# Attention with part of its exponentials on VectorE: a polynomial shared with GpSimd, and 30 key tiles instead of 27

## The chip, the cores and the metric

The kernel runs on one core of a Trainium2 chip. A core has TensorE (PE, with its weight loads as PEld), ScalarE (ACT), VectorE (DVE), GpSimd (POOL) and SyncE (SP, which issues DMAs). The metric is the device time of one execution in microseconds (us), given as the median of the runs.

## The reference

A cross-attention of 1024 queries over 6404 keys, 16 heads of 8 channels, and then a small mixture of experts. What matters here, cut down:

```
q = (layernorm(x) @ Wq + bq)          # 1024 x 128, 16 heads of 8
k, v = ctx @ Wk + bk, ctx @ Wv + bv   # 6404 x 128
attn = softmax(clip(q @ k.T * 8**-0.5, -1e4, 1e4))
x = x + (attn @ v) @ Wo + bo
x = x + a * (gelu(ln(x) @ W1m + b1m) @ W2m + b2m) + (1 - a) * experts(ln(x))
```

The work is in exp over 16 x 1024 x 6404 scores.

## The kernel before

The context is transposed and projected first, until about 53 us. Then comes the attention loop. It has eight passes; a pass is one group of four heads and one half of the queries (512 columns). The keys form 50 full tiles of 128 and a tail of 4. A (pass, key tile) is a step of four chunks, one for each head, of 128 keys by 512 queries. Three chunks make a tile of the loop: TensorE computes their scores into one of two PSUM tensors `ps` (L1058, the four heads in four row groups of the array), ScalarE takes exp of all 1536 columns in one instruction (L514), and TensorE adds the values of the steps that are complete (L1122, the four heads beside each other) into the pass's bank `po`. So in three of four tiles there is a values step and in one there is none. Two tiles of scores are in flight.

Some steps go to VectorE instead, by a list written out in the code, `D_PLAN`: pass, key tile, the four tiles of the loop at which TensorE makes the score of one head (a "spare score", in the `po` bank that the running pass doesn't use), the order of the heads, and the tile at which the values are added. VectorE makes exp by range reduction and a polynomial of degree five in three factors. For each spare score there is `u` (L764, adds a magic number and so rounds) and `f` (L767, the remainder), 512 columns each, after which the bank is free (`spare_taken`). Two scores make a pair of 1024 columns, on which `pair_until` runs six stages: 1 `e`, the shift of u into an exponent (L783); 2 `q1` = (f + A1) f (L792, and once for each key tile `vd`, L790); 3 `q2` = (f + A2) f (L794); 4 `p1` = (q1 + B1) e (L797); 5 `p2` = (q2 + B2) p1 (L800); 6 the last, (f - R0) p2 (L803), which signals `d_ready`. The stages of a pair are laid between u and f of the next pair's scores (`split_exponent`). TensorE must not make a spare score before VectorE has taken the one before it (`spare_job`, wait on `spare_taken`), and as its queue is in order, score tiles and values wait behind that.

At the end of a pass VectorE copies the sums out (`take_sums`, L746), TensorE transposes them into the spare bank (L1080, a "token job" in the same list of spare jobs), and VectorE divides (`normalise`, L738 and L739). Before, the pair begun is carried to stage 6 ahead of that. After pass 6 the first half of the queries is finished during pass 7: projection, layer norm, first main layer (`first_half_main`).

GpSimd has nothing to do in the loop but the power that gives the layer norm's rstd of the first half (L471). In the tail TensorE and VectorE hand each other the second half: transposes (L1151), normalise (L739), transposes (L1014), projection (L1021), residual and statistics, rstd by GpSimd, xn (L583), transposes (L1028), first layers (L1197), and `second_layer(0, 0)`, the second main layer of the first half, after the projection and ahead of L1028 (L1224, L1216).

The loop stands in an If on a range flag; its Else is a general path that these inputs don't take.

## Time and profile before

| | us |
|---|---|
| median of 3 runs | 810.94 |
| lowest, highest | 809.8, 810.98 |
| profiled execution | 812.0 |
| its span, first to last instruction | 810.3 |
| mean granted TensorE clock | 0.985 |

| engine | busy us | share of the span |
|---|---|---|
| TensorE matmuls | 732.8 | 90% |
| ScalarE | 726.7 | 90% |
| VectorE | 551.3 | 68% |
| GpSimd | 20.7 | 3% |

Busy time is not time on the path. A matmul's end is modelled and matmuls overlap, so TensorE's share says little; what tells is who waits for whom, and how long the engine that is waited for leaves no gap.

### The profile page before, as it was taken

What the parts mean: (1) busy time and instruction counts of PE and PEld (TensorE: products, weight loads), DVE (VectorE), ACT (ScalarE), POOL (GpSimd) and SP (SyncE); (2) the same over time, 40 slices, a digit from 0 to 9 for tenths busy, and PEclk for the clock granted to TensorE, in tenths of its full rate; (3) what the DMA queues carried; (4) which work ended last, traced back from release to release, by engine and by line L of the source; (5) the groups of instructions that cost most, each with busy time, mean ns of one, the idle gap of its engine ahead of it and who ended that gap; (6) DMA issues with size and microseconds to landing.
All of it is one profiled execution on the core that took longest, in us unless ns stands there. A gap on an engine that the chain in (4) does not pass through costs nothing.

```text
span 810.3 us, 13099 instructions
## 1 busy us (share of the span) xinstructions
PE 732.8 (90%) x5386; PEld 217.2 (27%) x5386; DVE 551.3 (68%) x760; ACT 726.7 (90%) x587; POOL 20.7 (3%) x36
## 2 busy tenths in 40 slices
PE   5988899999998998999989999899899999998798
PEld 3642222222222222222212222222222222222457
DVE  5634499798877988699759977898769884100220
ACT  3769999999999998999979999999899998999451
POOL 8000000000000000000000000000000000000000
PEclk9989999999999999999999999999999999999999
DMA  5259110011110000111100000111100000000010
GB/s 186 104 151 291 57 42 1 26 42 33 34 34 1 1 2 10 40 33 34 50 1 1 2 1 18 49 33 33 34 1 2 1 1 1 1 1 1 4 53 27
DMA packets 15325, 29.05 MB, mean 36 GB/s; under 512 B 2439, under 2 KB 5885, under 8 KB 15261
## 3 DMA queue, kind: packets, MB, share of 16 engines
q1 hardware_dynamic: 13562, 26.86, 10.8%
q8 instruction: 45, 0.74, 0.4%
q10 hardware_dynamic: 1218, 0.64, 0.3%
q0 software_dynamic: 480, 0.66, 0.3%
q14 instruction: 20, 0.16, 0.1%
HBM read 20.02 MB, written 8.13 MB: 35 GB/s over the span
## 4 chain that ended last, share of the span: by engine, by line
PE 47%; ACT 21%; issue 18%; DVE 8%; DMA 4%; SPq 1%; POOLq 0%; POOL 0%; DVEq 0%; ACTq 0%
PE po L1122 25%; ACT region_ctxT L514 20%; PE ps L1058 13%; DMA k_dram<-kparts 3%; PE ps L1197 2%; PE po L1216 1%; PE ps L950 1%; DVE dres L800 1%; DVE dres L797 1%; PE po L961 1%; DMA region_ctx<-in_ctx 1%; PE ps L938 1%; DVE dres L803 1%; DVE xn L583 1%; DVE dres L792 1%
## 5 line engine op out<-in xcount | busy, mean ns | idle before, releaser
L514 ACT ACTIVATE region_ctxT<-ps 128x1536 f32<-128x1536 f32 x500 | 680.0, 1531 | 21.2 <-PE ps L1058 21.0
L1122 PE MATMUL po<-region_ctxT,v 128*9 128x512 f32 x2984 | 393.6, 600 | 0.9 <-ACT region_ctxT L514 0.5
L1058 PE MATMUL ps<-qst,region_k 32*128 32x512 f32 x1492 | 252.9, 496 | 45.7 <-ACT region_ctxT L514 45.1
L1058 PEld LDWEIGHTS ps<-qst,region_k 32*128 32x128 f32 x1492 | 96.8, 182 | 420.4 <-ACT region_ctxT L514 398.9
L764 DVE TENSOR_SCALAR region_kT<-po 128x512 f32<-128x512 f32 x108 | 74.2, 687 | 92.2 <-PE po L1058 92.0
L767 DVE SCALAR_TENSOR_TENSOR region_kT<-region_kT,po 128x512 f32<-128x512 f32 x108 | 73.6, 681 | 0.7
L1122 PEld LDWEIGHTS po<-region_ctxT,v 128*9 128x9 f32 x2984 | 44.4, 88 | 94.2 <-issue 90.8
L803 DVE SCALAR_TENSOR_TENSOR dres<-region_kT,dres 128x1024 f32<-128x1024 f32 x54 | 66.2, 1225 | 1.8
L800 DVE SCALAR_TENSOR_TENSOR dres<-region_kT,dres 128x1024 f32<-128x1024 f32 x54 | 65.9, 1220 | 0.5
L792 DVE SCALAR_TENSOR_TENSOR dres<-region_kT 128x1024 f32<-128x1024 f32 x54 | 65.8, 1218 | 0.0
L794 DVE SCALAR_TENSOR_TENSOR region_kT<-region_kT 128x1024 f32<-128x1024 f32 x54 | 65.8, 1218 | 0.0
L797 DVE SCALAR_TENSOR_TENSOR dres<-dres,region_kT 128x1024 f32<-128x1024 f32 x54 | 65.7, 1216 | 0.0
L1058 PE MATMUL po<-qst,region_k 32*128 32x512 f32 x108 | 53.5, 495 | 3.9 <-DVE xn L739 3.0
L783 DVE TENSOR_SCALAR region_kT<-region_kT 128x1024 uint32<-128x1024 uint32 x54 | 36.9, 683 | 0.0
L746 DVE COPY region_kT<-po 128x512 f32<-128x512 f32 x8 | 5.5, 684 | 39.8 <-PE po L1108 39.8
L1122 PE MATMUL po<-dres,vd 128*9 128x512 f32 x216 | 28.6, 601 | 2.5 <-DVE dres L803 2.5
L1058 PEld LDWEIGHTS po<-qst,region_k 32*128 32x128 f32 x108 | 19.6, 181 | 5.8 <-DVE xn L739 3.4
L471 POOL TENSOR_TENSOR rstd<-rstd,powers 128x4 f32<-128x4 f32 x2 | 2.1, 1027 | 743.7 <-DVE rstd L578 743.7
L938 PE MATMUL ps<-ident,region_ctx 128*96 128x128 f32 x50 | 9.7, 332 | 7.3 <-DMA region_ctx<-in_ctx 7.3
L701 DVE TENSOR_SCALAR region_ctx<-po,b1T 128x512 f32<-128x512 f32 x4 | 3.0, 751 | 19.2 <-PE po L1037 19.2
L358 ACT ACTIVATE region_ctxT<-ps 96x512 f32<-96x512 f32 (+1 forms) x13 | 7.4, 572 | 9.4 <-PE ps L938 9.4
L624 DVE CAST kparts<-region_kT 128x640 fp32r<-128x640 f32 (+1 forms) x10 | 4.9, 493 | 15.4 <-DMA k_dram<-kparts 14.3
(191 smaller groups left out, 304.8 us busy)
## 6 DMA issues: line engine op xcount, KB each, us to landing
region_k<-k_dram SPq DMA_DIRECT2D x40, 320.0 KB, 3.3
k_dram<-kparts SPq DMA_DIRECT2D x18, 320.0 KB, 4.2
qst<-q_dram SPq DMA_DIRECT2D x16, 128.0 KB
region_ctx<-in_ctx SPq DMA_DIRECT2D x2, 624.0 KB, 9.3
q_dram<-region_k SPq DMA_DIRECT2D x2, 512.0 KB, 2.7
k_dram<-kparts SPq DMA_DIRECT2D x2, 322.0 KB, 5.3
region_ctx<-in_ctx SPq DMA_DIRECT2D x1, 576.0 KB, 7.4
xres<-in_x SPq DMA_DIRECT2D x1, 512.0 KB, 4.4
```

The source lines that it names most:

```text
L514: act.activation(probs[:, t % NPR, :], ps[t % NSB][:, :], ACT.Exp, scale=ESCALE).then_inc(exp_ready, 1)
L764: d_count(("u", c), v.tensor_scalar(du[:, i % 2, part], src, MAGIC, None, ALU.add))
L767: v.scalar_tensor_tensor(df[:, i % 2, part], du[:, i % 2, part], MAGIC, src, ALU.subtract, ALU.subtract).then_inc(spare_taken, 1)
L783: d_count(("e", i), v.tensor_scalar(u.bitcast(U32), u.bitcast(U32), 23, None, ALU.logical_shift_left))
L792: d_count(("q1", i), v.scalar_tensor_tensor(res, f, A1, f, ALU.add, ALU.mult))
L794: d_count(("q2", i), v.scalar_tensor_tensor(q, f, A2, f, ALU.add, ALU.mult))
L797: d_count(("p1", i), v.scalar_tensor_tensor(res, res, B1, u, ALU.add, ALU.mult))
L800: d_count(("p2", i), v.scalar_tensor_tensor(res, q, B2, res, ALU.add, ALU.mult))
L803: v.scalar_tensor_tensor(res, f, R0, res, ALU.subtract, ALU.mult).then_inc(d_ready, 1)
L938: last = tr(dst[:, at:at + P], ctx_sb[:, t, :], ident[:, :])
L1058: return mm(dst, kst[r, kt * P:(kt + 1) * P], qst[r, g, queries], start=True, stop=True)
L1122: last = mm(dst[QUAD * j:QUAD * j + V9, :], w, src, start=first, stop=last_one, skip_group_check=True)
```

## The change

Three things in the loop and one in the tail.

- The plan has 30 key tiles on VectorE instead of 27, in passes 0 to 7: 1, 4, 5, 4, 5, 4, 5, 2. The loop has 496 tiles instead of 500. The first spare score is at tile 29 instead of 21; often three tiles lie between two spare scores; two key tiles are in pass 7, the last with scores at tiles 466 to 477 and values at 485. Of the 59 distances between the first scores of one pair and the next, 34 are 6 tiles and six are 5.
- GpSimd makes q1 in two instructions on 1024 columns, `res = f + A1` and `res = res * f`, when both f of a pair are there (`first_factor`, semaphore `factor_ready`). VectorE's p1 waits for it. The power of L471 is placed between the factors.
- Ahead of a token job's normalising, the pair begun is carried on by at most `BETWEEN` = 2 stages and goes on afterwards. `D_GAP`, by which a pair was finished at once where the next score was over 6 tiles away, is gone; only the last pair is finished at once.
- In the tail the second main layer of the first half is cut into its four row tiles (`second_main`): one after the transposes L1151, one after L1014, two after the projection; then ten matmuls of 128 x 128 whose result isn't used (`IDLE`), ahead of the transposes L1028.

```diff
--- before.py
+++ after.py
@@ -60,8 +60,10 @@
 MIX_BANK = 5
 NORM_GAP = 2
 EPI_GAPS = [2, 2, 6, 2, 2, 2, 2]
-D_GAP = 6
+BETWEEN = 2
 OUT_TILES = [(0, QT // 2), (QT // 2, 3 * QT // 4), (3 * QT // 4, QT)]
+
+IDLE = 10
 ALPHA_COL = C + (E + 1) * CB
 assert FULL % NSEG == 0
 
@@ -82,33 +84,36 @@
 
 
 D_PLAN = [
-    (0, 44, (21, 23, 28, 30), (0, 2, 1, 3), 44),
-    (0, 49, (34, 37, 40, 43), (3, 0, 1, 2), 56),
-    (1, 49, (47, 50, 53, 60), (2, 3, 0, 1), 71),
-    (1, 48, (63, 70, 72, 77), (1, 2, 0, 3), 91),
...
-    (6, 47, (405, 408, 411, 418), (2, 3, 0, 1), 430),
-    (7, 49, (420, 425, 427, 433), (3, 2, 0, 1), 449),
+    (0, 49, (29, 31, 34, 36), (0, 2, 3, 1), 48),
+    (1, 49, (39, 42, 45, 52), (2, 3, 0, 1), 71),
+    (1, 48, (55, 58, 61, 64), (2, 3, 0, 1), 79),
+    (1, 47, (70, 72, 75, 81), (2, 0, 1, 3), 91),
+    (1, 46, (84, 87, 90, 93), (0, 1, 2, 3), 107),
+    (2, 14, (96, 99, 102, 105), (0, 1, 2, 3), 134),
...
+    (6, 47, (406, 410, 413, 416), (1, 0, 2, 3), 426),
+    (7, 49, (419, 422, 425, 428), (0, 1, 2, 3), 473),
+    (7, 48, (466, 468, 471, 477), (0, 2, 3, 1), 485),
 ]
 DKT = [[kt for p, kt, *_ in D_PLAN if p == q] for q in range(NP)]
 STEPS = [(p, kt) for p in range(NP) for kt in range(FULL + 1) if kt not in DKT[p]]
@@ -151,8 +156,8 @@
 
 
 def tile_of_segment(p, s):
-    return max(c for c, (n, _) in enumerate(CHUNKS)
-               if STEPS[n][0] == p and (STEPS[n][1] < FULL and STEPS[n][1] // SEG_T == s)) // CPT
+    return max((c for c, (n, _) in enumerate(CHUNKS)
+                if STEPS[n][0] == p and (STEPS[n][1] < FULL and STEPS[n][1] // SEG_T == s)), default=0) // CPT
 
 
 def spare_of_segment(g, s):
@@ -301,6 +306,7 @@
         kst_in = [sem(f"kst_in{s}") for s in range(NSEG)]
         bqs_ready, vtail_ready, powers_ready = sem("bqs_ready"), sem("vtail_ready"), sem("powers_ready")
         spare_psum, spare_taken, d_step, d_ready = sem("spare_psum"), sem("spare_taken"), sem("d_step"), sem("d_ready")
+        factor_ready = sem("factor_ready")
         pre_psum, pre_taken, main0_ready = sem("pre_psum"), sem("pre_taken"), sem("main0_ready")
         bsumb_psum, bsumb_taken = sem("bsumb_psum"), sem("bsumb_taken")
         scores_ready, exp_ready, pv_done, o_taken = sem("scores_ready"), sem("exp_ready"), sem("pv_done"), sem("o_taken")
@@ -465,10 +471,38 @@
             pool.wait_ge(powers_ready, 1)
             pool.memset(euler[:, :], math.e).then_inc(powers_ready, 1)
             pool.wait_ge(powers_ready, 2)
-            for n in range(NHALF):
+
+            first_power = [True]
+
+            def power(n):
                 pool.wait_ge(var_ready, 2 + n)
                 r = slice(n * QT // 2, (n + 1) * QT // 2)
                 pool.tensor_tensor(rstd[:, 3, r], rstd[:, 0, r], powers[:, 0:QT // 2], ALU.pow).then_inc(std_ready, 1)
+
+            def first_factor(i):
+
+                d, half = divmod(i, 2)
+                res = dres[:, d % 2, half * 2 * BANK:(half + 1) * 2 * BANK]
+                pool.wait_ge(spare_taken, SPARE_OF["score", 2 * i + 1] + 1)
+                if d >= 2:
+                    pool.wait_ge(pv_done, VALUES_OF_D[d - 2] + 1)
+                pool.tensor_scalar(res, df[:, i % 2, :], A1, None, ALU.add).then_inc(factor_ready, 1)
+                pool.wait_ge(factor_ready, 2 * i + 1)
+                pool.tensor_tensor(res, res, df[:, i % 2, :], ALU.mult).then_inc(factor_ready, 1)
+
+            pool.wait_ge(flag_ready, 1)
+            safe = pool.value_load(flag[0:1, 0:1], min_val=0, max_val=1)
+            with pool.If(safe != 0):
+                for i in range(len(D_PLAN) * GH // 2):
+                    if SPARE_OF["score", 2 * i + 1] > SPARE_OF["tokens", LAST_OF_HALF[0]] and first_power[0]:
+                        power(0)
+                        first_power[0] = False
+                    first_factor(i)
+                if first_power[0]:
+                    power(0)
+            with pool.Else():
+                power(0)
+            power(1)
             pool.wait_ge(msum_ready, 2)
             pool.tensor_tensor(gate[0:1, 2, :], euler[:, :], gate[0:1, 1, :], ALU.pow).then_inc(exp_gate, 1)
 
@@ -789,11 +823,11 @@
                                 heads = slice(GH * PASSES[p][0], GH * (PASSES[p][0] + 1))
                                 v.tensor_scalar(vd[:, d % 2, :].rearrange("p (h m) -> p h m", m=V9), v9[:, kt, heads, :],
                                                 C5, None, ALU.mult)
-                            d_count(("q1", i), v.scalar_tensor_tensor(res, f, A1, f, ALU.add, ALU.mult))
                         elif d_stage[i] == 3:
                             d_count(("q2", i), v.scalar_tensor_tensor(q, f, A2, f, ALU.add, ALU.mult))
                         elif d_stage[i] == 4:
-                            dve.wait_ge(d_step, max(d_mark["q1", i], d_mark["e", i]))
+                            dve.wait_ge(factor_ready, 2 * (i + 1))
+                            dve.wait_ge(d_step, d_mark["e", i])
                             d_count(("p1", i), v.scalar_tensor_tensor(res, res, B1, u, ALU.add, ALU.mult))
                         elif d_stage[i] == 5:
                             dve.wait_ge(d_step, max(d_mark["p1", i], d_mark["q2", i]))
@@ -807,11 +841,12 @@
                     if kind == "score":
                         split_exponent(i, n)
                         pairs = (i + 1) // 2
-                        if n + 1 == len(SPARE) or SPARE[n + 1][1] == "score" and SPARE[n + 1][0] > SPARE[n][0] + D_GAP:
+                        if pairs == len(d_stage):
                             pair_until(pairs - 1, 6)
                     else:
                         take_sums(i)
-                        pair_until(pairs - 1, 6)
+                        if pairs:
+                            pair_until(pairs - 1, min(6, d_stage[pairs - 1] + BETWEEN))
                         dve.wait_ge(spare_psum, n + 1)
                         ins = normalise(i, po[1 - pv_bank(i + 1)][:, :])
                         ins.then_inc(spare_taken, 1)
@@ -1021,6 +1056,22 @@
                     last = mm(dst[:, i * P:(i + 1) * P], attT[:, t * P:(t + 1) * P], wo_sb[:, :], start=True, stop=True)
                 last.then_inc(y_psum, 1)
 
+            def ffn_sum(t):
+
+                n = max(n for n, (t0, _) in enumerate(OUT_TILES) if t0 <= t)
+                a = t - OUT_TILES[n][0]
+                return [po[0], po[1], bank(4)][n][:, a * P:(a + 1) * P], a == 0
+
+            def second_main(t):
+
+                if t == 0:
+                    pe.wait_ge(main0_ready, 1)
+                    pe.wait_ge(w2_scaled, 1)
+                dst, first = ffn_sum(t)
+                for cb in range(CB):
+                    mm(dst, hid[0][:, cb, t * P:(t + 1) * P], w2m_sb[:, cb, :],
+                       start=(cb == 0 and first), stop=False, skip_group_check=True)
+
             def xn_transpose(n, dst):
 
                 pe.wait_ge(xn_ready, QT + (n + 1) * QT // 2)
@@ -1150,9 +1201,13 @@
                 for a in range(QT // 2):
                     last = tr(bank(0)[:, a * P:(a + 1) * P], oraw[:, (NP - 1) % 2, a * P:(a + 1) * P], ident[:, :])
                 last.then_inc(tok_psum, 1)
+                second_main(0)
                 pe.wait_ge(attention_done, NHALF)
                 att_transpose(1, bank(4))
+                second_main(1)
                 project_out(1, bank(5))
+                for t in range(2, QT // 2):
+                    second_main(t)
             with pe.Else():
                 with pe.Fori(0, H) as h:
                     with pe.Fori(0, QT) as t:
@@ -1186,6 +1241,8 @@
                     first_main(cb)
                 att_transpose(1, bank(4))
                 project_out(1, bank(5))
+                for t in range(QT // 2):
+                    second_main(t)
 
             def first_layer(e, steps):
                 for r in steps:
@@ -1197,17 +1254,8 @@
                     mm(bank(n % 4), w,
                        xnT[:, half * BANK:(half + 1) * BANK], start=True, stop=True).then_inc(hid_psum, 1)
 
-            def ffn_sum(t):
-
-                n = max(n for n, (t0, _) in enumerate(OUT_TILES) if t0 <= t)
-                a = t - OUT_TILES[n][0]
-                return [po[0], po[1], bank(4)][n][:, a * P:(a + 1) * P], a == 0
-
             def second_layer(e, half):
-                if e == 0 and half == 0:
-                    pe.wait_ge(main0_ready, 1)
-                else:
-                    pe.wait_ge(hid_ready, e * CB * NHALF + CB * half)
+                pe.wait_ge(hid_ready, e * CB * NHALF + CB * half)
                 pe.wait_ge(w2_scaled, e + 1)
                 w2 = w2m_sb if e == 0 else w2s[:, e - 1, :, :]
                 for t in range(half * QT // 2, (half + 1) * QT // 2):
@@ -1221,7 +1269,8 @@
                     last.then_inc(ffn2_done, 1)
 
 
-            second_layer(0, 0)
+            for _ in range(IDLE):
+                mm(bank(3, P, P), ident[:, :], ones[:, :], start=True, stop=True)
             xn_transpose(1, bank(4))
             pe.wait_ge(xnT_ready, 2 * NHALF)
             first_layer(0, range(CB, CB + 1))
```

## Rows read from the trace of the kernel before

**Rows 1.** The page's first part: busy us, share of the span, count.
```profile
PE 732.8 (90%) x5386; PEld 217.2 (27%) x5386; DVE 551.3 (68%) x760; ACT 726.7 (90%) x587; POOL 20.7 (3%) x36
```

**Rows 2.** The page's groups: line, engine, forms, count, busy, mean ns, idle, releaser.
```profile
L514 ACT ACTIVATE region_ctxT<-ps 128x1536 f32<-128x1536 f32 x500 | 680.0, 1531 | 21.2 <-PE ps L1058 21.0
...
L794 DVE SCALAR_TENSOR_TENSOR region_kT<-region_kT 128x1024 f32<-128x1024 f32 x54 | 65.8, 1218 | 0.0
...
L783 DVE TENSOR_SCALAR region_kT<-region_kT 128x1024 uint32<-128x1024 uint32 x54 | 36.9, 683 | 0.0
```

**Rows 3.** ScalarE's timeline: start us, length us, line, forms, count, idle before.
```profile
90.94 137.83 ACT L514 ACTIVATE region_ctxT<-ps 128x1536 f32<-128x1536 f32 x102 [0.92 <-PE ps L1058]
229.70 79.56 ACT L514 ACTIVATE region_ctxT<-ps 128x1536 f32<-128x1536 f32 x59 [0.92 <-PE ps L1058]
...
319.11 5.68 ACT L514 ACTIVATE region_ctxT<-ps 128x1536 f32<-128x1536 f32 x4 [1.17 <-PE ps L1058]
326.05 71.85 ACT L514 ACTIVATE region_ctxT<-ps 128x1536 f32<-128x1536 f32 x53 [1.26 <-PE ps L1058]
...
415.34 1.45 ACT L514 ACTIVATE region_ctxT<-ps 128x1536 f32<-128x1536 f32 x1 [4.53 <-PE ps L1058]
...
674.73 1.45 ACT L514 ACTIVATE region_ctxT<-ps 128x1536 f32<-128x1536 f32 x1 [1.20 <-PE ps L1058]
```

**Rows 4.** Timeline of TensorE, then VectorE, within 429 to 446 us.
```profile
435.14 0.50 PE L1058 MATMUL ps<-qst,region_k 32*128 32x512 f32 x3
435.15 0.50 PE L1058 MATMUL po<-qst,region_k 32*128 32x512 f32 x1
435.58 1.05 PE L1122 MATMUL po<-region_ctxT,v 128*9 128x512 f32 x8
436.56 0.50 PE L1058 MATMUL ps<-qst,region_k 32*128 32x512 f32 x3
437.69 0.50 PE L1058 MATMUL ps<-qst,region_k 32*128 32x512 f32 x3 [0.64 <-ACT region_ctxT L514]
...
432.38 0.68 DVE L764 TENSOR_SCALAR region_kT<-po 128x512 f32<-128x512 f32 x1
...
434.18 1.22 DVE L792 SCALAR_TENSOR_TENSOR dres<-region_kT 128x1024 f32<-128x1024 f32 x1
435.32 1.22 DVE L794 SCALAR_TENSOR_TENSOR region_kT<-region_kT 128x1024 f32<-128x1024 f32 x1
...
441.18 0.68 DVE L764 TENSOR_SCALAR region_kT<-po 128x512 f32<-128x512 f32 x1
```

**Rows 5.** Timeline of TensorE at the end of a pass, 409 to 420 us.
```profile
412.21 0.53 PE L1058 MATMUL po<-qst,region_k 32*128 32x512 f32 x1 [3.04 <-DVE xn L739]
...
412.67 1.90 PE L1122 MATMUL po<-region_ctxT,v 128*9 128x512 f32 x8
```

**Rows 6.** One line's durations; VectorE's and GpSimd's timeline in the first 18 us.
```profile
L583 DVE TENSOR_SCALAR xn<-xres,mv,rstd x16: 327/345/2091, 12.5 to 766.3; 128x128 f32<-128x128 f32 x16
...
12.48 5.23 DVE L583 TENSOR_SCALAR xn<-xres,mv,rstd 128x128 f32<-128x128 f32 x8
...
5.73 1.64 DVE L569 BATCH_NORM_STATS2 stats<-xres 128x6 f32<-128x128 f32 x8 [5.73 <-DMA xres<-in_x]
...
2.03 5.45 POOL L444 MEMSET region_ctxT<- 1x6432 f32 x1
```

**Rows 7.** GpSimd's groups by line and form.
```profile
L448 POOL MEMSET ktail<- 128x512 f32 x1 | 0.5, 525 | 0.1
...
L471 POOL TENSOR_TENSOR rstd<-rstd,powers 128x4 f32<-128x4 f32 x2 | 2.1, 1027 | 743.7 <-DVE rstd L578 743.7
```

**Rows 8.** Timeline of the tail, 762 to 769 us.
```profile
762.94 5.44 PE L1216 MATMUL po<-w2m_sb,region_kT 128*128 128x128 f32 x32 [2.33 <-issue]
...
765.53 1.11 DVE L583 TENSOR_SCALAR xn<-xres,mv,rstd 128x128 f32<-128x128 f32 x4 [2.67 <-issue]
...
768.21 0.60 PE L1028 MATMUL ps<-ident,xn 128*128 128x128 f32 x4
```

42 rows, old and new, of the table D_PLAN are left out of this document.

## Prediction, written before the changed kernel was run

> **What bounds the kernel now.** Five views, in this order. First the page's busy shares [rows 1]: PE and ACT are both at 90%, DVE at 68%. Shares don't decide between two such engines, so next the groups by line [rows 2]: the exponentials of L514 fill 680.0 us and wait for PE 21.0 us and for little else. Third ACT's timeline [rows 3]: the exponentials stand in long runs almost without a gap; 102 of them fill 137.83 us, so one tile costs 137.83 / 102 = 1.351 us. ACT sets the pace of the loop; the 21 us are all that others add. Fourth, PE and DVE in a stretch where a key tile is on VectorE [rows 4]: a tile with values and a spare score takes PE 436.56 - 435.14 = 1.42 us, and in the next, without values, it waits 0.64 us for ACT, so it has little room but some; DVE has none there: from one u to the same u of the next pair 441.18 - 432.38 = 8.80 us without idle, and PE's next spare score waits for it. Last the tail, where DVE, PE and ACT take turns [rows 8].
>
> **Four exponential tiles fewer.** Three more key tiles on DVE take 12 chunks from ACT: 500 tiles become 496. 4 x 1.351 = 5.4 us, on ACT, which is the path: -5.4. PE's sum is unchanged: the scores and values are made anyway; a spare score costs it next to nothing where it starts beside a score tile (435.14 and 435.15 in [rows 4]), and the values of a key tile on DVE fill a tile that has none. Over 12 tiles PE needs 10 x 1.42 + 2 x 0.5 = 15.2 us against ACT's 16.2, so PE stays hidden; were the cover gone, each us would be paid in full.
>
> **DVE with one step less.** The step from q1 to q2 is 435.32 - 434.18 = 1.14 us [rows 4]. Without q1 a pair costs 8.80 - 1.14 = 7.66 us, and a key tile 2 x 7.66 + 0.1 (vd) = 15.4. The plan gives 12 tiles or 16.2 us where it is densest (before: 13 tiles, 17.6 us, for exactly 17.6 of work). 34 of the 59 distances from pair to pair are 6 tiles (8.1 us for 7.66) and six are 5 tiles (6.75); elsewhere there are 7 to 14 tiles. Net: DVE keeps the pace with 0.4 us to spare a pair, if nothing lengthens its steps. The new wait is factor_ready ahead of p1; behind it on DVE stand p1, f, p2 and the last step, and for f waits PE's next spare score. GpSimd has, from the end of f to p1, p2 + last + u + e + f + q2 + u = 1.25 + 1.15 + 0.60 + 0.60 + 0.59 + 1.13 + 0.60 = 5.9 us (starts in the view of [rows 4], f of the second score to the u of the next pair's second).
>
> **What GpSimd needs.** The trace has no such operation. Its write of 512 columns took 0.53 us [rows 7]: 1024 columns with one input come to some 1.1 us. For two inputs the bounds are 1.1 (inputs read together) and 3.2 (twice that, and the 1.03 us that four columns took in L471 [rows 7]); I take 2.1, one read after the other. In all 3.3 us with the hops, between 2.2 and 4.4: below 5.9, so the wait itself costs nothing. The Trainium skill (GPSIMD Engine Reference, Elementwise — side-by-side cycle accounting) gives 4497 ns for a two-input add of 2048 columns; an estimate from that page for half of it is 2.25 us, and would alter nothing here.
>
> **The port they share.** In [rows 6] DVE's eight L583 scalings, from SBUF to SBUF, took 5.23 us beside GpSimd's DMA issues and writes, single ones up to 2091 ns, where the median of all 16 is 345 ns and four in the tail, without GpSimd, took 1.11 us [rows 8]. Statistics beside GpSimd's long write did not suffer: eight in 1.64 us against a GpSimd write of 5.45. The shift e is of the first kind: 683 ns for 1024 columns, little more than half of what a two-input step takes [rows 2]. It starts 3.0 us after f, GpSimd ends after 3.3 to 3.5: about 0.4 us of waiting, just the slack of a pair. I put +2 us on it (0 to +6; no gain is possible from waiting). The five-times larger question is the two-input steps q2, p1, p2 and last. No row shows one beside a GpSimd instruction that reads SBUF, so this is bounded by nothing (as the statistics) and full exclusion (as L583); I take nothing, since they don't run at the doubled rate at which the trace shows the blocking, and keep the other end as the first rival.
>
> **Pass ends.** Before, a pair begun is finished ahead of the normalising: PE's spare score starts at 412.21, after 3.04 us of waiting for the normalising of L739, and the next values step takes 1.90 us [rows 5] instead of 1.05 [rows 4], by the granted clock at the lower level. ACT lost 4.53 us. The same kind: 1.17 and 1.26 at 319.11 and 326.05, the same pair of gaps once more two passes later, and 1.20 at 674.73 [rows 3]; and 0.92 at 90.94, where the first spare scores of the plan, from tile 21, stood behind a DVE busy with the key tail; the new plan starts at tile 29. Sum 4.53 + 2 x 2.43 + 1.20 + 0.92 = 11.5 us. With at most two steps ahead of the normalising, most of this goes. What is late next is PE: the remaining gaps of about 0.9 at pass ends (229.70 in [rows 3]) come from the tail step, which costs PE a full values step for a third of a tile, and stay. As the new plan is denser around these ends, I take -9, between -4 and -11.5.
>
> **The tail.** PE ran the first half of the main layer from 762.94 in 5.44 us, after 2.33 us in which it waited for nothing shown, and the transposes followed at 768.21, though DVE's xn was ready at 765.53 + 1.11 = 766.64 [rows 8]: PE is late by 1.5 us. A pass took 5.44 / 32 = 0.17 us there; with the clock up (1.05 against 1.90 us for one step, above) I take 0.12. Now two of the four tiles fill PE's waits in the hand-overs with DVE (8 passes or 0.95 us each against waits a little shorter: each pushes the path by some 0.2 us), two follow the projection at once, and ten small matmuls, 20 passes or 2.3 to 3.4 us, stand ahead of the transposes. Projection ends 762.94 - 2.33 + 0.4 = 761.0, two tiles 762.9, the gap of 2.3 us 765.2, ten matmuls 767.5 to 768.6. Against 768.2: -0.5, between -1 and +0.6. GpSimd's rstd moves behind the factors of its queue; the last factor before it is older than the token job that starts the chain to it, so nothing waits.
>
> **Sum.** Profiled execution 812.0 us (span 810.3), against a median of 810.94. 812.0 - 5.4 - 9 + 2 - 0.5 = 799.1; less the 1.1 us by which the profiled one stood above the median: 798.0. Own range: -11.5, -1 and no contention give 793.0; -4, +6, +0.6 give 808.1.
>
> **Rivals.** (1) *The port excludes the two-input steps too.* For it: L583 [rows 6], and that DVE has only 0.4 us to spare. Against it: nothing in the trace, which is silent. Price: if GpSimd's first instruction starts under u and the second under f, it holds back e by 0.5 and q2 by 0.5 to 1.5 us: 8.7 to 9.7 us a pair; if it slips in after p2, it holds back the last step by 1.1 and e by 1.5: 10.3. Over 8.1 us that is 0.6 to 2.2 us in 34 pairs, over 6.75 us 2.0 to 3.5 in six: +32 to +96, and the time 828 to 892, most likely about 855. It turns slower than before from 8.5 us a pair on, where the excess eats the gain. The Trainium skill (SBUF — State Buffer, Who interferes with whom) has this as a rule: a VectorE instruction with two SBUF inputs contends with a GpSimd instruction that reads SBUF, and the later one waits for the whole of the other. By that rule the time is this rival's; no row here shows it. (2) *Only the gain of the tiles.* New gaps at the denser pass ends take the place of the old ones: 812.0 - 1.1 - 5.4 + 2 = 807.5, 804 to 813. (3) *Only the shift contends, but GpSimd is slow* (4.4 us): e waits 1.4 us, 1.0 over the slack in 40 pairs, some of it in gaps: +10 to +35, 808 to 833.
>
> **How the numbers follow.** Forecast 0.47, rival 1 0.33, rival 2 0.10, rival 3 0.10. A measurement of this kernel tells 0.2% from no change, 809.3 to 812.6. Faster: 0.47 + 0.07 + 0.01 = 0.55; same: 0.02 + 0.02 = 0.04; slower: 0.01 + 0.07 + 0.33 = 0.41. The likeliest case alone: 793 to 808. The range from 791 to 858 takes in that case, rivals 2 and 3, and a little over half of rival 1, and leaves out a little under 2 in 10.
>
> **What would show it.** L514 x496 at 1.35 us and idle before it near 12 us instead of 21.0: tiles and pass ends right. L792's former work as two GpSimd groups x60, 1.1 and 2.1 us. The means of L783 and of the two-input steps unchanged at 683 and 1218 ns: no contention; 1.5 us and more in their mean, with PE's spare score waiting for L767 and L514's idle in tens of us: rival 1. Idle at pass ends unchanged: rival 2. What makes the forecast wrong is a pair over 8.1 us on DVE.

## The result, and the profile after

| | before | after |
|---|---|---|
| median of 3 runs, us | 810.94 | 872.24 |
| lowest, highest | 809.8, 810.98 | 872.16, 873.3 |
| span of the profiled execution | 810.3 | 871.5 |
| mean granted TensorE clock | 0.985 | 0.947 |

The changed kernel takes 1.0758 times as long (95% interval 1.0734 to 1.0783): 61 us slower, where 798.0 was forecast with a range up to 858. The first rival, 828 to 892, holds the result.

The page's first part and groups of the kernel after, to be set beside [rows 1] and [rows 2]:

```profile
PE 780.5 (90%) x5406; PEld 226.3 (26%) x5406; DVE 662.6 (76%) x763; ACT 730.7 (84%) x583; POOL 400.1 (46%) x156
...
L548 ACT ACTIVATE region_ctxT<-ps 128x1536 f32<-128x1536 f32 x496 | 684.2, 1483 | 79.3 <-PE ps L1109 79.0
L489 POOL TENSOR_SCALAR dres<-region_kT 128x1024 f32<-128x1024 f32 x60 | 219.3, 3656 | 376.8 <-DVE region_kT L801 368.5
L491 POOL TENSOR_TENSOR dres<-dres,region_kT 128x1024 f32<-128x1024 f32 x60 | 160.0, 2666 | 5.0
...
L827 DVE SCALAR_TENSOR_TENSOR region_kT<-region_kT 128x1024 f32<-128x1024 f32 x60 | 114.5, 1909 | 0.0
L837 DVE SCALAR_TENSOR_TENSOR dres<-region_kT,dres 128x1024 f32<-128x1024 f32 x60 | 114.3, 1906 | 2.0
...
L834 DVE SCALAR_TENSOR_TENSOR dres<-region_kT,dres 128x1024 f32<-128x1024 f32 x60 | 72.8, 1214 | 0.1
L831 DVE SCALAR_TENSOR_TENSOR dres<-dres,region_kT 128x1024 f32<-128x1024 f32 x60 | 72.7, 1211 | 1.7 <-POOL dres L491 1.7
L817 DVE TENSOR_SCALAR region_kT<-region_kT 128x1024 uint32<-128x1024 uint32 x60 | 51.3, 855 | 0.0
L824 DVE TENSOR_SCALAR vd<-v 128x36 f32<-128x36 f32 x30 | 42.8, 1427 | 0.0
```

ACT, which set the pace before, now waits 79 us for PE, and DVE's groups say why: q2 (L827) and the last step (L837) rose from 1.22 to 1.91 us, the small `vd` (L824) took 1.43, while p1 and p2 stand at 1.21. The wait for the new semaphore is 1.7 us in the whole run (L831 behind POOL), so GpSimd's result is not late; its work is in the way. PE's part is one row of the waits (waited for: us in total, times, longest): its spare scores wait for f.

```profile
PE po L1109 <- DVE region_kT L801: 27.2, 36, 1.5
```

VectorE's timeline, then GpSimd's, in a dense stretch (start us, length us):

```profile
499.74 0.68 DVE L798 TENSOR_SCALAR region_kT<-po 128x512 f32<-128x512 f32 x1
...
501.54 1.74 DVE L824 TENSOR_SCALAR vd<-v 128x36 f32<-128x36 f32 x1
503.20 1.21 DVE L827 SCALAR_TENSOR_TENSOR region_kT<-region_kT 128x1024 f32<-128x1024 f32 x1
...
506.85 1.22 DVE L834 SCALAR_TENSOR_TENSOR dres<-region_kT,dres 128x1024 f32<-128x1024 f32 x1
508.10 1.94 DVE L837 SCALAR_TENSOR_TENSOR dres<-region_kT,dres 128x1024 f32<-128x1024 f32 x1
509.96 0.68 DVE L798 TENSOR_SCALAR region_kT<-po 128x512 f32<-128x512 f32 x1
510.56 0.68 DVE L817 TENSOR_SCALAR region_kT<-region_kT 128x1024 uint32<-128x1024 uint32 x1
511.16 0.68 DVE L801 SCALAR_TENSOR_TENSOR region_kT<-region_kT,po 128x512 f32<-128x512 f32 x1
511.76 2.79 DVE L827 SCALAR_TENSOR_TENSOR region_kT<-region_kT 128x1024 f32<-128x1024 f32 x1
...
519.92 0.68 DVE L798 TENSOR_SCALAR region_kT<-po 128x512 f32<-128x512 f32 x1
...
507.02 3.67 POOL L489 TENSOR_SCALAR dres<-region_kT 128x1024 f32<-128x1024 f32 x1 [3.78 <-DVE region_kT L801]
510.78 2.69 POOL L491 TENSOR_TENSOR dres<-dres,region_kT 128x1024 f32<-128x1024 f32 x1
```

From u to u a pair takes 10.22 and 9.96 us, not 7.66. The last step is 0.72 us longer beside the one-input instruction (1.94 against 1.22), and q2 1.57 longer beside the two-input one (2.79 against 1.22), or `vd` is in its place (1.74 for 0.18). 7.66 + 2.29 = 9.95.

Where the 61.2 us of span lie: the first exponential starts 0.8 earlier (52.27 against 53.11). The loop, from there to the table load behind the last one, takes 815.21 - 52.27 = 762.9 against 753.74 - 53.11 = 700.6: +62.3, of which +58.1 is idle ahead of the exponentials (79.3 - 21.2) and +4.2 their busy time. That should have fallen by 5.4; exponentials that stand alone take 1.45 us and not 1.35, and there are now many. The tail takes 56.3 against 56.6.

A gap costs PE more than its own length. Behind a wait for the last step, in a stretch with a granted clock of 0.53, near the lower of its two levels (500 to 502 us), a values step took 1.81 us; at the upper level, 1.00 (504 to 511 us), it takes 1.05:

```profile
499.97 1.81 PE L1173 MATMUL po<-dres,vd 128*9 128x512 f32 x8 [1.31 <-DVE dres L837]
```

How much of the 61 us comes in this way no run separates.

### The profile page after: what moved, and what is told of

Same layout as the page of the kernel before. It is cut to its first block, busy times and chain, and to the rows that moved or that the text cites. A ratio compares the mean times of both kernels' runs of the same rounds, so it can differ in the third digit from the quotient of the medians.

```text
span 871.5 us, 13388 instructions
## 1 busy us (share of the span) xinstructions
PE 780.5 (90%) x5406; PEld 226.3 (26%) x5406; DVE 662.6 (76%) x763; ACT 730.7 (84%) x583; POOL 400.1 (46%) x156
## 4 chain that ended last, share of the span: by engine, by line
PE 39%; DVE 32%; issue 19%; ACT 8%; DMA 1%; POOL 1%; POOLq 0%; SPq 0%; ACTq 0%
PE po L1173 19%; PE ps L1109 10%; ACT region_ctxT L548 7%; DVE dres L831 6%; DVE dres L834 5%; DVE region_kT L801 5%; DVE region_kT L798 5%; DVE region_kT L827 3%; DVE region_kT L817 3%; DVE dres L837 2%; PE ps L1254 2%; DVE vd L824 1%; PE po L1264 1%; PE po L996 1%; PE ps L985 1%
## 5 line engine op out<-in xcount | busy, mean ns | idle before, releaser
L548 ACT ACTIVATE region_ctxT<-ps 128x1536 f32<-128x1536 f32 x496 | 684.2, 1483 | 79.3 <-PE ps L1109 79.0
L1173 PE MATMUL po<-region_ctxT,v 128*9 128x512 f32 x2960 | 410.3, 628 | 2.3 <-ACT region_ctxT L548 1.4
L489 POOL TENSOR_SCALAR dres<-region_kT 128x1024 f32<-128x1024 f32 x60 | 219.3, 3656 | 376.8 <-DVE region_kT L801 368.5
L491 POOL TENSOR_TENSOR dres<-dres,region_kT 128x1024 f32<-128x1024 f32 x60 | 160.0, 2666 | 5.0
L798 DVE TENSOR_SCALAR region_kT<-po 128x512 f32<-128x512 f32 x120 | 81.8, 682 | 59.5 <-PE po L1109 59.3
L837 DVE SCALAR_TENSOR_TENSOR dres<-region_kT,dres 128x1024 f32<-128x1024 f32 x60 | 114.3, 1906 | 2.0
L827 DVE SCALAR_TENSOR_TENSOR region_kT<-region_kT 128x1024 f32<-128x1024 f32 x60 | 114.5, 1909 | 0.0
L801 DVE SCALAR_TENSOR_TENSOR region_kT<-region_kT,po 128x512 f32<-128x512 f32 x120 | 81.1, 676 | 0.3
L831 DVE SCALAR_TENSOR_TENSOR dres<-dres,region_kT 128x1024 f32<-128x1024 f32 x60 | 72.7, 1211 | 1.7 <-POOL dres L491 1.7
L834 DVE SCALAR_TENSOR_TENSOR dres<-region_kT,dres 128x1024 f32<-128x1024 f32 x60 | 72.8, 1214 | 0.1
L817 DVE TENSOR_SCALAR region_kT<-region_kT 128x1024 uint32<-128x1024 uint32 x60 | 51.3, 855 | 0.0
L824 DVE TENSOR_SCALAR vd<-v 128x36 f32<-128x36 f32 x30 | 42.8, 1427 | 0.0
```

Source lines behind the costliest of these rows:

```text
L489: pool.tensor_scalar(res, df[:, i % 2, :], A1, None, ALU.add).then_inc(factor_ready, 1)
L491: pool.tensor_tensor(res, res, df[:, i % 2, :], ALU.mult).then_inc(factor_ready, 1)
L548: act.activation(probs[:, t % NPR, :], ps[t % NSB][:, :], ACT.Exp, scale=ESCALE).then_inc(exp_ready, 1)
L798: d_count(("u", c), v.tensor_scalar(du[:, i % 2, part], src, MAGIC, None, ALU.add))
L801: v.scalar_tensor_tensor(df[:, i % 2, part], du[:, i % 2, part], MAGIC, src, ALU.subtract, ALU.subtract).then_inc(spare_taken, 1)
L817: d_count(("e", i), v.tensor_scalar(u.bitcast(U32), u.bitcast(U32), 23, None, ALU.logical_shift_left))
```

## The experiments

The theory after the result is rival 1: GpSimd's reads hold up VectorE's two-input steps. Against it stand that the denser plan or the new wait costs the time, and that the loss goes by how long GpSimd works. Each expectation says by itself which theories it sets against each other.

**Without the factor.** GpSimd doesn't make q1, and its buffer is set to 1.0 once, so the first factor is left out of the polynomial.

```diff
+            pool.memset(dres[:, :, :], 1.0).then_inc(vones_ready, 1)
...
-                    first_factor(i)
...
-                            dve.wait_ge(factor_ready, 2 * (i + 1))
```

> The changed kernel without GpSimd's two instructions and without the wait for them; the first quadratic factor is left out (res is set to 1 once), all else, the plan of 30 key tiles too, is as changed. Theory A (GpSimd's reads hold the port and so lengthen VectorE's two-input steps): a pair costs 7.66 us again, L837 and L827 go back from 1.91 to 1.22 us, ScalarE's idle before L548 falls from 79 to 10 to 15 us, time 796 to 803 us. Rival B (the plan of 30 is too dense for TensorE or for the pass ends, whatever GpSimd does): ScalarE's idle stays above 40 us, time over 830 us.

788.2 us (ratio to before 0.9707, 95% interval 0.9687 to 0.9728; the intervals are given in the same way below). That is 8 us under the written range: the idle ahead of the exponentials is 7.2 us, not 10 to 15. L837 and L828, the former L827, are back at 1.22 us, so the rival of a plan that is too dense falls.

**GpSimd writes only.** The wait and both instructions stay, but the instructions only write 1.0 (the first factor is left out again).

```diff
-                pool.tensor_scalar(res, df[:, i % 2, :], A1, None, ALU.add).then_inc(factor_ready, 1)
+                pool.memset(res, 1.0).then_inc(factor_ready, 1)
                 pool.wait_ge(factor_ready, 2 * i + 1)
-                pool.tensor_tensor(res, res, df[:, i % 2, :], ALU.mult).then_inc(factor_ready, 1)
+                pool.memset(res, 1.0).then_inc(factor_ready, 1)
```

> The changed kernel with GpSimd's two instructions replaced by two writes of 1.0 to the same 1024 columns (so the first factor is left out); the wait for GpSimd stays. Theory A: GpSimd reads nothing, so the two-input steps keep 1.22 us; only the shift e and vd, which run at the doubled rate, can be held up, by under 1.1 us a pair and mostly within the slack: 797 to 812 us. Rival C (any GpSimd instruction holds up VectorE's two-input steps): L837 or L827 at 1.6 us and more, time over 825 us.

787.38 us (0.969, 0.967 to 0.9711), 10 us under the written range. Its groups:

```profile
L548 ACT ACTIVATE region_ctxT<-ps 128x1536 f32<-128x1536 f32 x496 | 671.4, 1554 | 7.4 <-PE ps L1109 7.3
L837 DVE SCALAR_TENSOR_TENSOR dres<-region_kT,dres 128x1024 f32<-128x1024 f32 x60 | 73.5, 1225 | 2.0
L827 DVE SCALAR_TENSOR_TENSOR region_kT<-region_kT 128x1024 f32<-128x1024 f32 x60 | 73.2, 1219 | 0.0
```

Wait and semaphore cost nothing (787.4 against 788.2 without them), and VectorE's steps are at their old length. 872.24 - 787.38 = 84.9 us come with GpSimd's reading instructions in place of its writes. (The kernel before stood at 810.94 beside the first figure and at 811.86 beside the second, so this is good to about 1 us.) The writes are shorter too (0.95 us each against 3.66 and 2.67); the two runs with one GpSimd instruction each, below, tell length and reading apart.

**q1 back on VectorE**, with the new plan, pass ends and tail.

```diff
-                    first_factor(i)
...
+                            d_count(("q1", i), v.scalar_tensor_tensor(res, f, A1, f, ALU.add, ALU.mult))
```

> The changed kernel with the first factor q1 back on VectorE; 30 key tiles, pass ends and tail as changed. Theory A: a pair costs 8.80 us, 0.7 us over the 8.1 us of 34 pairs and 2.05 over the 6.75 of six, that is up to 36 us of idle beside the 10 to 15 of the run without a factor: 815 to 835 us, well under 872. Rival B: near 872 us, since the plan costs the time.

809.46 us (0.9977, 0.9959 to 0.9995), below what was expected: VectorE at 8.8 us a pair follows the denser plan with many small gaps. Idle ahead of the exponentials is 21.4 us, PE's spare scores wait 7.5 us for f.

The total is that of the kernel before (21.2), but its parts are not. Single gaps of more than 0.8 us came to 17.1 us before and come to 4.1 here; those of 0.1 to 0.8 us rose from 3.3 to 16.2. Where the kernel before stood still for 4.53 us at 415 us, and for 1.17 and 1.26 us between 580 and 588 us, ACT now runs through:

```profile
395.26 47.54 ACT L547 ACTIVATE region_ctxT<-ps 128x1536 f32<-128x1536 f32 x35 [0.39 <-PE ps L1108]
...
550.96 63.97 ACT L547 ACTIVATE region_ctxT<-ps 128x1536 f32<-128x1536 f32 x47 [0.41 <-PE ps L1108]
```

**GpSimd alone**, in the kernel before with its 27 key tiles: q1 moves, nothing else.

> The kernel before with one part of the change alone: q1 made by GpSimd, in its two instructions. 27 key tiles, pass ends and tail as before. Theory A: a pair costs 8.80 - 1.14 + 2.4 (0.72 on the last step, 1.57 on q2 or on vd) = 10.0 us against plan distances of 6 tiles (8.1 us) in 18 pairs and 7 (9.45) in 21: 1.9 x 18 + 0.6 x 21 = 47 us, so 845 to 865 us. Rival B (it is the denser plan together with GpSimd): 811 to 825 us, since this plan is wider.

843.45 us (1.041, 1.0355 to 1.0464). The loss is there without the denser plan, a little under the 845 expected; idle ahead of the exponentials is 46.2 us. This trace also has the price of GpSimd's product in the kernel, res by f from two buffers, with nothing beside it: VectorE did nothing from 90.45 to 95.36 us.

```profile
93.41 2.37 POOL L485 TENSOR_TENSOR dres<-dres,region_kT 128x1024 f32<-128x1024 f32 x1
```

**The cost by itself.** Behind the kernel before, a series of instructions on 1024 columns from SBUF to SBUF, each engine waiting for its own last one. Alone on VectorE: two-input 1.23 us (2 in 2.49), reduction 1.22, one-input scaling 0.71 (2 in 1.42). Then with GpSimd beside it; GpSimd's two-input instruction here multiplies one buffer by itself.

> The kernel before, with a series of instructions on 1024 columns behind its end: each kind alone and then VectorE and GpSimd at once. Alone I expect 1.1 us for GpSimd's one-input instruction and 2.1 to 2.7 for the two-input one, 1.2 and 0.68 us for VectorE's two-input and doubled ones. Theory A: VectorE's two-input instruction is stretched by GpSimd's one- and two-input instruction and not by a write; its one-input reduction by none; the doubled one by all. And GpSimd's one-input instruction gets to 3 us and more beside a row of two-input instructions. Rival C: the write stretches the two-input ones too. Rival D (sharing, not exclusion): every instruction is stretched by a constant share, whichever began first.

GpSimd alone, then VectorE's five beside one one-input, one two-input instruction, three writes, and five reductions beside both kinds:

```profile
811.93 5.63 POOL L490 TENSOR_SCALAR dres<-dres 128x1024 f32<-128x1024 f32 x2 [5.21 <-DVE gen L972]
817.65 3.86 POOL L491 TENSOR_TENSOR dres<-dres 128x1024 f32<-128x1024 f32 x2
821.57 1.96 POOL L492 MEMSET dres<- 128x1024 f32 x2
...
823.87 6.98 DVE L957 SCALAR_TENSOR_TENSOR dres<-dres 128x1024 f32<-128x1024 f32 x5 [11.78 <-POOL euler L504]
...
831.13 7.83 DVE L957 SCALAR_TENSOR_TENSOR dres<-dres 128x1024 f32<-128x1024 f32 x5
...
839.25 6.26 DVE L957 SCALAR_TENSOR_TENSOR dres<-dres 128x1024 f32<-128x1024 f32 x5
...
845.80 6.24 DVE L958 TENSOR_REDUCE gen<-dres 128x1 f32<-128x1024 f32 x5
```

Five two-input steps take some 6.25 us undisturbed. Beside the one-input instruction they lose 0.73 us, beside the two-input one 1.58; beside writes, and as reductions beside either kind, nothing. In the kernel the losses are 0.72 and 1.57 us. GpSimd's one-input instruction takes 2.8 us alone, its two-input one 1.93: the longer one holds VectorE up less.

In two more sets VectorE begins with a reduction of 512 columns, so that its two two-input steps start 0.67 us behind GpSimd's instruction:

```profile
864.51 3.56 DVE L957 SCALAR_TENSOR_TENSOR dres<-dres 128x1024 f32<-128x1024 f32 x2
...
869.08 2.71 DVE L957 SCALAR_TENSOR_TENSOR dres<-dres 128x1024 f32<-128x1024 f32 x2
...
863.84 1.89 POOL L491 TENSOR_TENSOR dres<-dres 128x1024 f32<-128x1024 f32 x1 [0.89 <-DVE gen L972]
...
868.42 2.77 POOL L490 TENSOR_SCALAR dres<-dres 128x1024 f32<-128x1024 f32 x1 [2.38 <-DVE gen L972]
```

Over 2.49 us that is a loss of 1.07 beside the two-input instruction and 0.22 beside the one-input one, 0.51 less than before in both, and GpSimd's instruction isn't lengthened. In the earlier sets VectorE was first by 0.05 us; there GpSimd's instruction grew by 1.0 us, about the rest of VectorE's step, and then held up the next step for the whole 0.73 or 1.58. So whoever comes first goes through and the other waits, and what GpSimd holds is a stretch near the start of its instruction: 0.73 us of 2.77 for one input, 1.58 of 1.89 for two. Sharing by a constant rate, rival D of the expectation, falls.

That the 1.58 us of the series and the 1.57 of the kernel agree is in part chance. In the kernel the product takes 2.37 us alone and not 1.89, 0.48 longer. If it holds by as much longer (an estimate, 1.58 + 0.48 = 2.06 us) and has to wait for the end of e (510.56 + 0.68 = 511.24 in the timeline above), it holds until 513.30; f, which ran in that time, stayed at 0.68, and q2, begun at 511.76, had to wait 1.54. Measured are 1.57.

**One GpSimd instruction at a time.** The changed kernel with only one of the two; q1 lacks the product by f in the first, and is f x f in the second.

```diff
+                pool.tensor_scalar(res, df[:, i % 2, :], A1, None, ALU.add).then_inc(factor_ready, 2)
```

> The changed kernel with only GpSimd's one-input instruction, res = f + A1 (the product by f is left out, so q1 is wrong and the work less by one GpSimd instruction). Theory A: each GpSimd instruction keeps VectorE's two-input steps back only while it reads, 0.72 us for the one-input one and 1.57 for the two-input one. A pair of scores then costs VectorE 7.66 + 0.72 = 8.38 us; over 8.1 us in 34 pairs and 6.75 in six that is 0.28 x 34 + 1.63 x 6 = 19 us on the 787.4 of the kernel in which GpSimd only writes: 807, 800 to 815. The last step or one other in its mean at 1.9 us, q2 and vd back near 1.2 and 0.2. Theory B, the loss goes by the length of the GpSimd instruction (3.66 against 2.67 us): it would cost more than half of the 85 us, 832 and more, and more than the product alone.

801.9 us (0.9895, 0.9876 to 0.9914).

```diff
+                pool.tensor_tensor(res, df[:, i % 2, :], df[:, i % 2, :], ALU.mult).then_inc(factor_ready, 2)
```

> The changed kernel with only one GpSimd instruction with two inputs, res = f * f in place of both (so q1 is wrong). Theory A: a pair costs 7.66 + 1.57 = 9.23 us; over 8.1 us in 34 pairs and 6.75 in six that is 1.13 x 34 + 2.48 x 6 = 53 us on 787.4: 841, 830 to 850. One two-input step lengthened by 1.5 us in each pair, the sum of the means of q2, p1, p2 and last up by about 1.6 us against 4 x 1.22. Theory B, the loss goes by the length of the instruction: less than half of the 85 us, 822 and less, and less than with the one-input instruction alone.

848.83 us (1.0471, 1.045 to 1.0492). The last step and GpSimd's instruction, of the first kernel and then of the second:

```profile
L835 DVE SCALAR_TENSOR_TENSOR dres<-region_kT,dres 128x1024 f32<-128x1024 f32 x60 | 114.4, 1906 | 2.0
L489 POOL TENSOR_SCALAR dres<-region_kT 128x1024 f32<-128x1024 f32 x60 | 215.5, 3591 | 475.5 <-DVE region_kT L799 412.4 <-issue 43.0 <-PE po L1171 20.1
```
```profile
L835 DVE SCALAR_TENSOR_TENSOR dres<-region_kT,dres 128x1024 f32<-128x1024 f32 x60 | 163.2, 2720 | 2.0
L489 POOL TENSOR_TENSOR dres<-region_kT 128x1024 f32<-128x1024 f32 x60 | 163.5, 2725 | 572.0 <-DVE region_kT L799 494.6 <-issue 57.0 <-PE po L1171 20.4
```

Over 787.4 that is +14.5 and +61.4 us; with both instructions in the kernel it was +84.9. In the dense stretch around 445 us a pair takes 8.46 us (442.04 to 450.50) in the one and 9.23 (439.52 to 448.75) in the other. The loss goes by what is held, not by how long GpSimd works: the 3.59 us instruction costs a quarter of what the 2.73 us one does. (A pair loses half as much, 0.73 against 1.58 us; the slack of 0.4 us a pair takes in the larger part of the small one.) The theory by length falls. The size came within the written ranges, 5 us under and 8 over their middle.

**Carrying alone**, with 27 key tiles: at most two steps ahead of the normalising, the rest right behind it.

```diff
-                        pair_until(pairs - 1, 6)
+                        if pairs:
+                            pair_until(pairs - 1, min(6, d_stage[pairs - 1] + BETWEEN))
...
+                        pair_until(pairs - 1, 6)
```

> The kernel before with one part alone: at a token job at most two steps of the pair begun come ahead of the normalising, and the rest right behind it (the changed kernel lets them wait longer; with this plan's due times that would not end). The prediction's term: the gaps of 4.53, twice 1.17 and 1.26, and 1.20 us go, up to 10.6 us: 801 to 806 us. If the gaps come from elsewhere: 811 us.

808.92 us (0.9981, 0.9955 to 1.0007): a miss, between the 801 to 806 of the one theory and the 811 of the other, and the noise doesn't part it from no change. The idle ahead of the exponentials is unchanged at 21.4 us. Where before one gap of 4.53 us stood [rows 3], ACT's timeline has three:

```profile
412.34 1.45 ACT L515 ACTIVATE region_ctxT<-ps 128x1536 f32<-128x1536 f32 x1 [1.92 <-PE ps L1061]
415.18 1.45 ACT L515 ACTIVATE region_ctxT<-ps 128x1536 f32<-128x1536 f32 x1 [1.39 <-PE ps L1061]
417.74 1.45 ACT L515 ACTIVATE region_ctxT<-ps 128x1536 f32<-128x1536 f32 x1 [1.10 <-PE ps L1061]
```

Their sum is 4.41. With the rest of the pair right behind the normalising, VectorE does the same work there and only in another order. The changed kernel lets that rest wait longer, which this run doesn't have.

**The tail alone**, with 27 key tiles:

> The kernel before with the tail alone: the four row tiles of the second main layer moved and ten idle matmuls. The transposes L1028 begin 1.0 to 1.6 us earlier after the last exponential, as in the changed kernel; if the expert weights land when they did, that is given back where TensorE waits for them: -0.3 to -1.5 us, 810 to 812 us.

808.91 us (0.9967, 0.9949 to 0.9985), somewhat better than written: the trace's tail is 1.4 us shorter. **Carrying and tail** together:

> Both together on 27 key tiles with q1 on VectorE. If they add: 800 to 805 us, faster than both kernels.

807.52 us (0.9948, 0.992 to 0.9977): the lowest time here of a kernel that computes everything. The two gains add as far as the noise lets one see (0.19% and 0.33%, together 0.52%), but the 800 to 805 us written for that case were missed, as carrying brought so little.

**Another plan.** 30 key tiles with q1 on VectorE and the pairs spaced by 13 tiles for two, its own 8.8 us, and once more with 0.1 tile more for each score. By their lists, spare scores fall between a pass's end and its normalising (tiles 66 and 310 in the first, 250 in the second), in the bank that holds the pass's sums, and overwrite them before they are copied out; the amount of work is the same, but these are not correct plans.

> q1 back on VectorE with pass ends and tail as changed and the same 30 key tiles, but the spare scores spaced for a pair of 8.8 us: 13 tiles from key tile to key tile instead of 12 or 16 by turns, from tile 26 on. Theory A: VectorE's work of 60 x 8.8 us fits into tiles 26 to 433, so ScalarE's idle falls from the 20.8 us of the run with q1 back to some 10 us and the single exponentials join again: 794 to 801 us, faster than both kernels. Rival B: at this density TensorE or the rounding to whole tiles leaves gaps whatever the spacing: 805 to 810 us.

> The same with 0.14 us more room for each spare score, so that half of the key tiles have 13 and half 14 tiles. If a little room saves the small waits of TensorE for VectorE, it is faster than the plan without by 1 to 3 us; if there are none, the same within 0.2%.

811.29 us (0.9998, 0.9982 to 1.0013) and 810.1 (0.9977, 0.9959 to 0.9996). The first misses both of its ranges; the second is 1.2 us less, within what was written, but the intervals overlap. Gaps of 0.1 to 0.8 us fell from 16.2 to 6.9 us in the first, but the idle is 24.3 us, and much of it stands behind pass ends; from ACT's timeline of the first:

```profile
151.82 1.45 ACT L547 ACTIVATE region_ctxT<-ps 128x1536 f32<-128x1536 f32 x1 [3.49 <-PE ps L1108]
...
496.19 1.45 ACT L547 ACTIVATE region_ctxT<-ps 128x1536 f32<-128x1536 f32 x1 [2.63 <-PE ps L1108]
499.56 1.45 ACT L547 ACTIVATE region_ctxT<-ps 128x1536 f32<-128x1536 f32 x1 [1.93 <-PE ps L1108]
```

These follow the ends of passes 0 and 4, the two at which a spare score is misplaced. So neither run settles what a correct plan with such spacing would take.

## Why the prediction was wrong

**What bounds the kernel: right.** VectorE's period for a pair was named as what decides, with 8.1 us as the limit. It came to 10.

**Four tiles, 5.4 us: borne out** where nothing disturbs: the exponentials' busy time fell by 8.6 us in the kernel that only writes, of which these are a part. **DVE with one step less, 7.66 us: right**; without contention the loop keeps the pace (787.4, idle 7.4).

**What GpSimd needs: mis-sized, without effect.** I took 1.1 us for one input and 2.1 for two, by a write's rate and a doubling; alone they take 2.8 and 1.93, and the kernel's product from two buffers 2.37. The write's rate didn't carry over to the instructions that compute, and the order is the other way round. In the kernel they take 3.66 and 2.67, since they are held up too. Their sum of 6.3 us with the hop is over the 5.9 I allowed, yet p1 waited 1.7 us in all: VectorE had been stretched by then. With VectorE stretched like this, GpSimd's length didn't matter, only what it reads.

**The port they share: the step that failed.** "I take nothing, since they don't run at the doubled rate" made an argument out of two rows, the statistics and L583 [rows 6], neither of which has two inputs from SBUF. The nearest fact would have been how many inputs come from SBUF: q2, p1, p2 and last have two; u reads PSUM alone and f one of its two inputs from PSUM, and they stayed at 682 and 676 ns. The term that was set to 0 measures 2.29 us a pair. Over the distances of the plan, (9.95 - 8.1) x 34 + (9.95 - 6.75) x 6 = 82 us, against 84.9 measured between reading and writing. Rival 1 had this formula and a pair of 8.7 to 10.3 us; its chance, 0.33, was too small, and its likeliest sum, 855, put 57 us on 798, where the runs show 84.9 on 787.4: the pair is at the upper end of its prices, and the kernel without the reading is faster than I had it. That it turns slower than before from 8.5 us a pair on doesn't follow from that formula, which gives (8.5 - 8.1) x 34 + (8.5 - 6.75) x 6 = 24 us there, more than the forecast's gain of 13; the point is at about 8.2. From the 787.4 that the runs show, it lies higher: at 8.46 us a pair the kernel took 801.9.

The Trainium skill (SBUF — State Buffer, Who interferes with whom) says that a two-input VectorE instruction contends with a GpSimd instruction that reads SBUF and not with one that writes; both halves hold here (7.83 and 6.98 against 6.26 for five). That the later one waits for the whole of the other, as I put the rule, doesn't: a 2.8 us instruction cost 0.73. It waits until the other's reading is through, and which of the two is the later one decides who waits, as the sets of the series with the later start show.

**The shift e: right in kind.** 855 ns for 683 in the mean, 0.17 x 60 = 10 us of busy time. It isn't spread evenly: 52 of the 60 took 0.7 us, as in the dense stretch above, and eight took 1.3 to 2.7. `vd` I had not looked at: 36 columns that wait 1.6 us for GpSimd; they wait in q2's place, so they add next to nothing. The four lengthenings together come to 0.69 + 0.69 + 0.17 + 0.62 = 2.2 us a pair (last, q2, e and half of vd, since there is one vd for two pairs).

**Pass ends: size off, and the place only in part.** Forecast -9 by carrying; measured -13.8 of idle in the kernel that only writes (21.2 to 7.4), and 3.2 us more because longer runs spare exponentials at 1.45 us (680.0 - 671.4 = 8.6, of which 5.4 are the tiles). Carrying alone, with the old plan and the rest of the pair right behind the normalising, gave nothing. With the new plan, where that rest may wait, the large gaps did go, without slack on VectorE (q1 back: 17.1 to 4.1 us in gaps over 0.8 us), as forecast. What it didn't have is that the denser plan puts 12.9 us of small gaps in their place, so that the sum of the idle stays at 21.4; these closed with VectorE's slack of over 1 us a pair (idle 7.4, small gaps 3.1), which I had entered as the condition of three more tiles and not as a gain of its own. Which part of closing the large gaps is the carrying and which the new places of the scores, and whether carrying is needed beside the slack, wasn't tried.

**The tail: right in size, by luck.** The forecast was -0.5 us and the tail is 0.3 shorter, but as the difference of two terms: one larger than forecast, one that I had at nothing. The transposes start 12.98 us after the last exponential (828.19 - 815.21), before 14.47 (768.21 - 753.74). Of these 1.5 us, 1.2 are given back: TensorE waits 1.33 us for the experts' weights, which land at nearly the same distance from the last exponential as before (24.7 and 24.9 us). They are asked for 1.2 us earlier (835.30 - 815.21 = 20.1 against 775.00 - 753.74 = 21.3), but the two transfers took 4.6 and 4.8 us to land instead of 2.9 and 3.3; why, no run shows. In the kernel with the tail alone that wait is 0.19 and the tail is 1.4 us shorter (809.1 - 753.95 = 55.15 against 56.56). How much stays depends on a DMA that no step of mine had.

## What to carry to other kernels

Before giving GpSimd part of VectorE's work, list VectorE's instructions there by how many inputs they read from SBUF. Here each GpSimd instruction that reads SBUF held up those with two, and the one-input ones at the doubled rate, even one of 36 columns, and the engine that was to be relieved lost more than it gave up (1.14 us handed over, 2.3 us paid). When no row shows two engines side by side in the form that is to run, neither bound can be taken as the likely value, and a short series of both, side by side, decides it before the kernel is changed. And a sum of idle time that stays the same says little: list the gaps by place and size, since large ones can have gone and small ones come.

## What the hardware showed

- GpSimd's one-input instruction with an immediate (1024 columns, 2.8 us alone) is slower than its product of a buffer by itself (1.93) or of two buffers (2.37), and a write takes 0.98.
- The hold goes with the kind of read and not with the length: 0.73 us for the first, 1.58 for the second, in the series and in the kernels with one GpSimd instruction (1.906 and 2.720 us for 1.22). A VectorE step that starts 0.67 us behind GpSimd's instruction loses 0.51 us less, 0.22 and 1.07. That the held stretch is the one in which GpSimd reads is my reading: it is shorter than the instruction, and a write has none.
- It works both ways: GpSimd's instructions grow to 3.80 and 2.92 us where VectorE's step was first by 0.05 us, and stay at 2.77 and 1.89 where they were first.
- A VectorE step of two inputs, one of them from PSUM, isn't held up: f stays at 0.68 us beside GpSimd's product (511.16 in the timeline of the changed kernel).
- VectorE's one-input steps at the doubled rate contend with writes too: five beside three GpSimd writes took 5.86 us, against 3.55 by 0.71 each, where two-input steps lost nothing.
